# Half-precision parts for a two-layer network and for the queries of a cross attention, in a six-stage transformer kernel on one core

## The reference

```python
# first cross attention: Q from the normalised tokens, K and V from the context, no softmax over keys
Q = Sq @ Wq_w.T + Wq_b            # 1024 x 256 times 256 x 1024
...
# second layer, self-attention block, after the attention:
x_norm2 = layer_norm(x, g2, beta2)
ffn = jax.nn.relu(x_norm2 @ W1 + b1) @ W2 + b2     # 256 -> 1024 -> 256
return x + ffn
```

## Time and profile before

| what | us |
|---|---|
| median of 3 runs | 1931.04 |
| lowest and highest | 1930.85, 1933.86 |
| the profiled execution | 1943.5 |
| its span, first to last instruction | 1941.8 |

### The profile page before, as it was taken

The page is one execution under the profiler, slowest core; times in us unless marked ns, Lnnn a source line. Parts: engine busy times, 40 slices in busy tenths (PEclk is TensorE's granted clock), DMA queues, the critical chain, the costliest instruction groups (busy, mean ns, idle before and its releaser), DMA issues.

```text
span 1941.8 us, 34714 instructions
## 1 busy us (share of the span) xinstructions
PE 1676.4 (86%) x13900; PEld 913.9 (47%) x13900; DVE 1316.1 (68%) x2014; ACT 1083.6 (56%) x1942; POOL 276.1 (14%) x248
## 2 busy tenths in 40 slices
PE   6988868999798999846999999999999679886877
PEld 4556645666566888521333333333333433462252
DVE  4223343381276888659999999999991686427867
ACT  3312112888643888311999999999999106311620
POOL 3223001898320000300000000000000000000000
PEclk9989989999888999875999999999999779886978
DMA  8123110899723766266433533543400070118100
GB/s 321 66 87 94 32 44 20 279 282 298 228 96 107 240 237 200 69 100 93 84 60 74 99 65 63 91 84 60 83 25 2 19 98 3 44 35 106 39 1 22
DMA packets 144653, 196.62 MB, mean 101 GB/s; under 512 B 34454, under 2 KB 109864, under 8 KB 140232
## 3 DMA queue, kind: packets, MB, share of 16 engines
q1 hardware_dynamic: 142764, 190.07, 38.1%
q0 software_dynamic: 1728, 4.33, 0.7%
HBM read 143.04 MB, written 51.00 MB: 100 GB/s over the span
## 4 chain that ended last, share of the span: by engine, by line
PE 43%; DVE 41%; issue 5%; POOL 4%; DMA 3%; ACT 2%; SPq 1%; another core or an unknown queue 1%; DVEq 0%; ACTq 0%; POOLq 0%
DVE mx_part L2200 28%; PE bank L1192 5%; PE pair L1234 5%; DVE mx L2309 3%; POOL k_part L2541 2%; PE bank L1045 2%; PE bank L1336 2%; PE pair L1395 2%; PE bank L252 2%; PE pair L1160 2%; PE pair L1147 2%; PE bank L1089 2%; DMA xT<-x_slots 2%; POOL c_lo L2528 2%; PE pair L1551 2%
## 5 line engine op out<-in xcount | busy, mean ns | idle before, releaser
L1743 ACT ACTIVATE pexp_all<-bank 128x512 f32<-128x512 f32 x1024 | 551.9, 595 | 97.9 <-PE bank L1350 84.5
L2200 DVE TENSOR_REDUCE mx_part<-pair 128x2 f32<-128x1024 f32 x512 | 583.0, 1213 | 16.6 <-PE pair L1322 14.2
L1336 PE MATMUL bank<-pexp_all,vst 128*17 128x256 f32 x4096 | 321.4, 386 | 6.0 <-issue 6.0
L1322 PE MATMUL pair<-kst,qs 49*128 49x512 f16 x1024 | 210.0, 407 | 44.7 <-DVE mx_part L2200 28.0
L1350 PE MATMUL bank<-qs,kst 52*128 52x256 f16 x2048 | 203.2, 271 | 0.0
L1322 PEld LDWEIGHTS pair<-kst,qs 49*128 49x128 f16 x1024 | 50.4, 93 | 273.2 <-DVE mx_part L2200 215.0
L1350 PEld LDWEIGHTS bank<-qs,kst 52*128 52x128 f16 x2048 | 120.7, 95 | 57.0 <-ACT pexp_all L1743 18.4
L1760 ACT ACTIVATE pexp_all<-bank 128x512 f32<-128x512 f32 x128 | 67.6, 595 | 120.5 <-PE bank L1458 120.3
L1336 PEld LDWEIGHTS bank<-pexp_all,vst 128*17 128x17 f32 x4096 | 68.6, 95 | 114.7 <-issue 105.3
L1677 ACT ACTIVATE hid_f<-bank,b 128x256 f32<-128x256 f32 (+1 forms) x152 | 78.6, 519 | 51.1 <-PE bank L1192 36.0
L1234 PE MATMUL pair<-w_hi,hid_hi 128*128 128x256 f16 x368 | 101.1, 275 | 3.2 <-issue 1.8
(11 more groups left out here) (323 smaller groups left out, 3042.5 us busy)
## 6 DMA issues: line engine op xcount, KB each, us to landing
w_f<-in_w_all SPq DMA_DIRECT2D x34, 1024.0 KB, 6.2
kst<-k_scr SPq DMA_DIRECT2D x192, 128.0 KB
v_scr<-v_st SPq DMA_DIRECT2D x64, 272.0 KB, 3.3
vst<-v_scr SPq DMA_DIRECT2D x16, 1088.0 KB, 5.6
ctx_sb<-in_ctx SPq DMA_DIRECT2D x16, 1024.0 KB, 5.0
cT<-in_ctxT SPq DMA_DIRECT2D x32, 512.0 KB, 5.6
k_scr<-k_part SPq DMA_DIRECT2D x128, 128.0 KB, 3.6
x_slots<-zeros SPq DMA_DIRECT2D x1, 3840.0 KB, 21.1
```

The source lines that it names most:

```text
L1322: last = pe.matmul(pair[n % 2][:, e * 512:(e + 1) * 512], qs[g % NBK][rws, p, qt * P:(qt + 1) * P], kst[g % NBK][rws, p, kb * 512:(kb + 1) ...
L1336: last = pe.matmul(bank[3][32 * h:32 * h + HV, 0:S], vst[g % 2][:, c, h * HV:(h + 1) * HV], unit_exp[n % NUE][:, p * S:(p + 1) * S], start ...
L1743: act.activation(unit_exp[n % NUE], bank[SCORE_BANKS[n % 3]], ACT.Exp, scale=SCALE).then_inc(s_exp, 1)
L2200: dve.tensor_reduce(mx_part[:, :, 2 * p + qt, kb], pair[n % 2][:, :].rearrange("p (e k) -> p e k", e=2), X_AXIS, ALU.max).then_inc(s_mx, 1)
```

## The change

The queries of the first cross attention and both layers of the network behind `sa5` are computed from half-precision parts, as the experts are.

- Queries: ScalarE makes the high parts of the weights (four pieces) before its copies of the transposes, and writes each transposed piece twice (fp32 and fp16). VectorE makes the low parts of weights and tokens after the second copy of the Gram matrix. The bias addition over `x` moves behind them. The parts lie in the memory of `tok` and `gw`, which is unused at that time (so the tile names of these instructions are `tok` and `gw`).
- Network: the weights are loaded behind the rows of maxima of batch 1 and split in the second pass of `sa5`, by the code that `sa6` had. The bias of the second layer is added there in quarters. `turn5` has two destinations. The hidden values go to four fp32 buffers `h5_f` and are split by VectorE; the addition of the attention's output to `x` stands in quarters between the first jobs.

```diff
-        turn0 = Turn(u, [(xT, None, None)])
+        turn0 = Turn(u, [(xT, None, None), (x0_part[:, 0], None, None)])
...
-        turn5 = Turn(tok, [(xT, "L1_attn_g2", "L1_attn_beta2")])
+        turn5 = Turn(tok, [(xT, "L1_attn_g2", "L1_attn_beta2"), (x5_part[0], "L1_attn_g2", "L1_attn_beta2")])
...
                 for b in range(B):
                     max_rows(b)
+                    if b == 1 and sa.turn == 0:
+                        sp.dma_start(r_f[:, 0:KT * HID].rearrange("p (k n) -> p k n", k=KT),
+                                     a["r_w1"].rearrange("(k p) n -> p k n", p=P)).then_inc(s_wa, 16)
+                        sp.dma_start(r_f[:, KT * HID:8 * 512].rearrange("p (m n) -> p m n", m=HM),
+                                     a["r_w2"].rearrange("(k p) n -> p k n", p=P)).then_inc(s_wa, 16)
...
-                turned(pe, turn0, half)
+                pe.wait_ge(s_q0p, 4 + KT * (half + 1))
...
                     for k in range(KT):
-                        last = pe.matmul(bank[2 + job % 2], w0q[:, k, m * P:(m + 1) * P],
-                                         xT[:, k, half * 512:(half + 1) * 512], start=(k == 0), stop=(k == KT - 1))
+                        for i, (w_, x_) in enumerate(((0, 0), (0, 1), (1, 0))):
+                            last = pe.matmul(bank[2 + job % 2], w0q_part[:, w_, k, m * P:(m + 1) * P],
+                                             x0_part[:, x_, k, half * 512:(half + 1) * 512],
+                                             start=(k == 0 and i == 0), stop=(k == KT - 1 and i == 2))
...
-                turned(pe, turn5, half)
+                pe.wait_ge(s_xlo, FIRST_INPUTS + KT * (half + 1))
...
-                        last = pe.matmul(bank[4 + job % 4], r_w1[:, k, m * P:(m + 1) * P],
-                                         xT[:, k, half * 512:(half + 1) * 512], start=(k == 0), stop=(k == KT - 1))
+                        for i, (w_, x_) in enumerate(((0, 0), (0, 1), (1, 0))):
+                            last = pe.matmul(bank[4 + job % 4], r_w1[w_][:, k, m * P:(m + 1) * P],
+                                             x5_part[x_][:, k, half * 512:(half + 1) * 512],
+                                             start=(k == 0 and i == 0), stop=(k == KT - 1 and i == 2))
...
-                pe.wait_ge(s_h5e, HM * (t // 4 + 1))
+                pe.wait_ge(s_hlo, FIRST_HIDDEN + HM * (t // 4 + 1))
...
+                    for i, (h_, w_) in enumerate(((0, 0), (0, 1), (1, 0))):
+                        last = pe.matmul(bank[2 + t % 2][:, 0:D], h5_part[h_][:, m, t * P:(t + 1) * P], r_w2[w_][:, m, :],
+                                         start=(m == 0 and i == 0), stop=(m == HM - 1 and i == 2))
...
+            act.wait_ge(s_wa, 32)
+            for i in range(4):
+                k, ns = i // 2, slice(i % 2 * 512, (i % 2 + 1) * 512)
+                act.activation(w0q_part[:, 0, k, ns], w0q[:, k, ns], ACT.Copy, scale=W_SCALE).then_inc(s_q0h, 1)
             act_turn(act, turn0)
...
                 for n in range(2 * SELF_STEPS):
-                    if sa.turn == 1 and n >= 32 and n % 4 == 0:
-                        last_weights_high((n - 32) // 4)
+                    if n >= 32 and n % 4 == 0:
+                        tail_weights_high(sa.turn, (n - 32) // 4)
...
                 act.wait_ge(s_h5, job + 1)
+                if job >= 4:
+                    act.wait_ge(s_hlo, FIRST_HIDDEN + job - 3)
+                act.activation(h5_f[:, job % 4, :], bank[4 + job % 4], ACT.Relu, bias=col("L1_attn_b1", job % HM),
+                               scale=1.0 / W_SCALE).then_inc(s_h5e, 1)
```

More of the change, by code:

```diff
@@ L2392, in _ @@
             dve_norm(dve, st, norm5, u, tok, measured=True)
-            st.link(dve.tensor_tensor(x[:, :, :], x[:, :, :], u[:, :, :], ALU.add))
-            st.settle()
-            st.link(dve.tensor_tensor(x[:, :, :], x[:, :, :], per_tile_rows("L1_attn_b2"), ALU.add))
+            inputs_low(turn5, x5_part)
+            for job in range(2 * HM):
+                half, m = divmod(job, HM)
+                hs = slice(half * 512, (half + 1) * 512)
+                dve.wait_ge(s_h5e, job + 1)
+                st.link(dve.tensor_copy(h5_part[0][:, m, hs], h5_f[:, job % 4, :]))
+                st.settle()
+                dve.tensor_tensor(h5_part[1][:, m, hs], h5_f[:, job % 4, :], h5_part[0][:, m, hs], ALU.subtract)\
+                    .then_inc(s_hlo, 1)
+                if job in (0, 2, 4, 6):
+                    ts = slice(job, job + 2)
+                    st.link(dve.tensor_tensor(x[:, ts, :], x[:, ts, :], u[:, ts, :], ALU.add))
             st.settle()
@@ L2431, in _ @@
                                          op0=ALU.mult, op1=ALU.add).then_inc(s_y6, 1)
[L2432 to L2436 removed]
+            inputs_low(turn7, x6_part)
             dve.wait_ge(s_y6, T)
```

122 lines of the change are left out of this document (71 added, 51 removed).

## The result

The changed kernel takes 1904.35 us, median of four (1898.27 to 1910.8), beside 1931.4 us for the kernel before, median of four beside it (1930.85 to 1933.86): a ratio of 0.9857, 95% interval 0.9831 to 0.9883, or 27 us less. Two more comparisons on other executions gave 0.9862 (0.9826 to 0.9897) and 0.9874 (0.9849 to 0.9900). The forecast was 18.4 us less, 1912.6, and its range ended at 1904.5, 0.15 us above the result. The direction was right, the size was not.

A forecast was written before the change was run, and what follows sets the result against it. TensorE was taken to bound the queries and the two layers, though TensorE and VectorE alternate overall. Gains 7.0 + 12.5 less 1.1 made 18.4 us, so 1931.0 became 1912.6 us, range 1904.5 to 1921.

The forecast's parts named there:

- Price of a product: TensorE's new streams: six half-precision products take 1.295 us against 1.72 per fp32 job; second layer 2.62 us a tile against 3.47.
- Queries: First cross attention: queries start at 36.2 instead of 36.52, next stage at 58.0 instead of 65.03, gaining 7.0 us.
- Self-attention ahead: +1.1: Self-attention before the two layers: carries eight weight pieces and four quarter additions, so 1.1 us longer.
- only TensorE bounds these stages: Queries and two layers: ScalarE only follows, and nothing else ends a wait of TensorE there.
- Rival (b): First of the two layers: VectorE's split sets the pace, 3.5 us more than TensorE's work, 1916.1 us; chance 0.08.
- Rival (c): All three new streams: they don't keep the full clock, up to 62.4 us more, 1975 us; chance 0.03.
- the case of the Trainium skill: Queries on two PSUM banks: 512-column products cycling through banks might lose and regain the clock repeatedly; weighed under slower streams.
- Two layers, start: Start of the two layers: moves from 1672.80 to 1673.6, 0.8 us later, at most 2 if copies don't overlap.
- I take 1.2: Start of the first layer's stream: 1.2 us lost to the low clock, between ends of 0.3 and 2.9.
- the old start was 36.52: Queries in the kernel before: start read at 36.52 us from the profiled timeline, making the new start 0.3 us earlier.
- rival (a): Batch rounds of the first cross attention: clock falls move, 7.1 us won (1905.5, chance 0.10) or lost (1919.7, chance 0.15).
- The base: Whole kernel: the same 18.4 us subtracted from the profiled execution (1943.5) and from the median (1931.0).

The follow-up runs named there:

- after2: The changed kernel run once more, unaltered, on another chip: 1920.0 us beside 1949.3 for the kernel before (0.9862).
- after3: The changed kernel run once more, unaltered, beside a shifted version of it: 1927.4 us beside 1952.2 for the kernel before (0.9874).
- mlp_second32: The changed kernel with the second of the two layers back in fp32 and no VectorE split between jobs: the pair takes 50.3 us, against 43.9.
- after_fill: The changed kernel with small dummy products in two waits of each batch round of the first cross attention: 1914.3 us (0.9850 against the kernel before).
- before_fill: The kernel before with the same small dummy products in two waits of each batch round: 1935.8 us (0.9954 against the kernel before).

## Why the prediction missed

**Right, to a few tenths.** Price of a product: six every 1.29 us, a tile every 2.62. Queries: start 36.42 (forecast 36.2), next stage 58.17 (58.0), gain 6.9 against 7.0 (against the profiled execution). "Self-attention ahead: +1.1": from the same exponential to the first gathered tile it is 22.82 us now and was 21.86, +0.96. The stage as a whole came out at only +0.2, because the profiled kernel before has a half-clock stretch shortly ahead of that exponential and the changed kernel has none there (the two windows show the same stretch of work, before and after); that won 0.9 us back. In the traces `after2` and `after3` the same interval is 22.82 us too.

```profile
1613.00:1624.00 11.00, 9.05 (x98) 3.21 (x98) 9.89 (x20) 5.51 (x12) 0.00 (x0) 0.84 0.02 4
```

```profile
1581.70:1592.70 11.00, 8.43 (x106) 3.15 (x106) 10.61 (x20) 6.37 (x13) 0.00 (x0) 1.00 0.02 5
```

The reading that only TensorE bounds these stages held. Rival (b), VectorE's split, is ruled out by `mlp_second32`. Rival (c) too: after its first ten products no product of the new streams in the two layers ran at the low clock, and in the profiled changed kernel the queries on two banks ran at 0.215 us from the first; the case of the Trainium skill that was weighed there (TensorE: Matmul & The Clock Gate, "A second HAM failure mode: psum-queue depth-cycling") did not occur.

**Terms mis-sized, small.** "Two layers, start" was +0.8 and measured +1.1 (ScalarE's eight copies came 0.67 us apart, not 0.55). "I take 1.2" for the clock was 2.1, ten slow products. Together the two layers gave 11.2 instead of 12.5.

**Two terms that were missing.** Behind the two layers 2.5 us were won from the clock, in code that the change leaves alone. And the queries won 1.3 us more on average than against the profiled execution, which had no fall at their start. The forecast asked about the clock only where instructions changed and in the batch rounds, and "the old start was 36.52" was taken from one execution. The sum of the stages is 6.9 + 11.2 - 0.2 + 2.5 = 20.4 against the profiled execution and 21.7 with the queries on average; `after_fill` against `before_fill` shows 20 to 21.5.

**The step that failed** is the treatment of rival (a): "The clock further back moves", at 0.10 for the better side and 0.15 for the worse, on the ground that "the clock at the first round is full now, which speaks against both by a little". The mechanism and its price (7.1 us for a round, measured 7.2) were right, and the trace after shows exactly this. The error was to take the round lengths of one execution as the kernel's own, a base from which it could get better or worse alike. The kernel before carries 8 to 9 us of falls in these rounds on average, and the most that any trace shows is 10.5, so there was far more room on the better side; even the execution read for the prediction lost 8.8 (53.2, 60.4 and 54.8 us), while the changed kernel, in its eight unshifted traces, loses 3.4. Some 5 of the 27 us come from here (8.3 less 3.4): 21.7 + 5 = 26.7, and the three ratios give 24.6, 26.9 and 27.6. The 5 us rest on one trace of each run; the times alone don't separate them from the noise. Why the two kernels draw different positions so often, and whether they would on further chips, stays open, so part of this gain may be luck.

**The base.** Subtracting the same gain from the profiled execution and from the median held. The 12.5 us between them are about the 15.3 us of "remote" waits in that execution, which come with either kernel and so don't enter the difference. The two chips with such waits give 24.6 and 26.9 us, and the first comparison 27.6.

## What to carry over

Before the sum is closed, go through every stretch with a granted clock under 1.00 in the trace, also in stages that the change doesn't touch, and ask whether a shift of a few microseconds can move it: here that was almost 9 of 27 us. A half-clock stretch seen in one execution is one draw; its price belongs into the range, on the side on which the draw was bad. A few dummy products in a wait of under 1 us cost nothing measurable here; they took away the falls of these rounds and, in all executions but one, most of the spread.

## What the hardware showed unexpectedly

- A wait of 0.8 to 1.0 us among small fp32 products is enough for a fall of the clock in one execution and not in the next, and the fall costs 1.6 or 7.2 us by where it comes.
- The same kernel on the same chip spreads over 17 us (1920.2 to 1937.2 in 21 executions); the five fastest have a mean clock of 0.920 to 0.924, the five slowest of 0.917 to 0.919.
- The kernel before took 15 to 22 us more on two other chips than on the first one, with waits on "remote" of up to 8.7 us in the expert part.
